# A decoder layer on one core: output sum by pairs of heads, expert weights in a ring of quarters, query and key copies on ScalarE

## The reference, cut to what matters

```python
q = (x @ w_q).reshape(b, n, HEADS, DIM_HEAD).transpose(0, 2, 1, 3)   # 8 heads of 64
k = (x @ w_k).reshape(b, n, HEADS, DIM_HEAD).transpose(0, 2, 1, 3)
gates = jax.nn.sigmoid((x @ w_gate).reshape(b, n, HEADS, EXPERTS).transpose(0, 2, 1, 3))
sel = jnp.argmax(gates, axis=-1)
gm = jax.nn.one_hot(sel, EXPERTS, dtype=x.dtype) * gates
values = jnp.einsum('bhne,ehdk,bnd->bhnk', gm, value_experts, x)
sim = jnp.einsum('bhid,bhjd->bhij', q * SCALE, k)                    # causal mask, then softmax
attn = jax.nn.softmax(sim, axis=-1)
out = jnp.einsum('bhij,bhjk->bhik', attn, values)
out = jnp.einsum('bhne,ehkd,bhnk->bhnd', gm, output_experts, out)
return out.sum(axis=1)
```

## Time and profile before

| | |
|---|---|
| median of 3 runs | 1032.64 us (1027.52 to 1032.67) |
| the profiled execution's own time | 1030.41 us |
| its span | 1028.6 us |
| mean granted TensorE clock | 0.97 |
| TensorE matmuls busy | 932.1 us (91%) |
| VectorE busy | 672.6 us (65%) |
| GpSimd busy | 397.9 us (39%) |
| ScalarE busy | 348.4 us (34%) |
| heads of the third layer | about 251 to 419 and 759 to 918 us |
| output sum | about 420 to 527 and 918 to 1025 us |

### The profile page before, as it was taken

The page is one execution under the profiler, slowest core; times in us unless marked ns, Lnnn a source line. Parts: engine busy times, 40 slices in busy tenths (PEclk is TensorE's granted clock), DMA queues, the critical chain, the costliest instruction groups (busy, mean ns, idle before and its releaser), DMA issues.

```text
span 1028.6 us, 15147 instructions
## 1 busy us (share of the span) xinstructions
PE 932.1 (91%) x5740; PEld 713.0 (69%) x5740; DVE 672.6 (65%) x1032; ACT 348.4 (34%) x634; POOL 397.9 (39%) x365
## 2 busy tenths in 40 slices
PE   6989899998889798689999999999989889885998
PEld 3578588886555455489975777888765556455998
DVE  4767575466455565898869556754754465768887
ACT  4545563111444445201124355610014454541000
POOL 6212231125666667635620032300045664782000
PEclk9999999999889899899999999999989999998999
DMA  6111002532453621445540000022330121131753
GB/s 203 46 63 62 1 1 69 178 100 71 146 162 99 234 59 44 121 150 179 174 134 1 1 1 1 2 89 82 103 103 21 22 60 25 42 94 44 220 178 123
DMA packets 39014, 90.18 MB, mean 88 GB/s; under 512 B 8975, under 2 KB 13775, under 8 KB 38943
## 3 DMA queue, kind: packets, MB, share of 16 engines
q1 hardware_dynamic: 36063, 79.79, 24.9%
q10 hardware_dynamic: 2880, 9.44, 4.0%
HBM read 61.35 MB, written 19.30 MB: 78 GB/s over the span
## 4 chain that ended last, share of the span: by engine, by line
PE 77%; DMA 8%; DVE 8%; issue 3%; ACT 3%; POOL 0%; SPq 0%; ACTq 0%; POOLq 0%; DVEq 0%
PE ps L1254 17%; PE ps L1602 10%; PE ps L1494 5%; PE ps L1478 5%; PE ps L1608 5%; DMA qq<-qq 5%; PE ps L1433 4%; PE ps L1520 4%; PE ps L1262 4%; PE ps L1385 3%; PE ps L1447 3%; PE ps L1400 2%; PE ps L1566 2%; PE ps L1567 2%; PE ps L1296 1%
## 5 line engine op out<-in xcount | busy, mean ns | idle before, releaser
L1116 DVE TENSOR_REDUCE region<-ps 128x1 f32<-128x512 f32 (+1 forms) x192 | 99.0, 551 | 105.1 <-PE ps L1497 102.4
L1602 PE MATMUL ps<-expert_hi,kst 128*128 128x256 f32 x512 | 128.1, 288 | 26.4 <-DVE kst L1200 24.8
L1169 DVE COPY_PREDICATED region<-region,ps 128x512 f32<-128x512 uint32 x112 | 82.0, 736 | 72.2 <-PE ps L1254 71.6
L1602 PE MATMUL ps<-expert_lo,kst 128*128 128x256 f32 x512 | 125.7, 282 | 0.0
L624 POOL TENSOR_TENSOR xT<-xT,region 128x896 f32<-128x896 f32 (+2 forms) x48 | 83.9, 1748 | 92.5 <-PE ps L1520 50.7
L1602 PEld LDWEIGHTS ps<-expert_hi,kst 128*128 128x128 f32 x512 | 98.1, 192 | 30.4 <-DVE kst L1200 22.3
L1254 PE MATMUL ps<-expert_hi,wide_hi 128*128 128x512 f32 x256 | 102.7, 401 | 0.0
L1494 PE MATMUL ps<-kst,qq 128*128 128x512 f32 (+1 forms) x192 | 74.8, 436 | 30.2 <-DMA qq<-qq 30.2
L1254 PE MATMUL ps<-expert_hi,wide_lo 128*128 128x512 f32 x256 | 100.1, 391 | 0.0
L1254 PE MATMUL ps<-expert_lo,wide_hi 128*128 128x512 f32 x256 | 99.8, 390 | 0.0
L1602 PEld LDWEIGHTS ps<-expert_lo,kst 128*128 128x128 f32 x512 | 98.5, 192 | 0.0
(11 more groups left out here) (163 smaller groups left out, 1953.4 us busy)
## 6 DMA issues: line engine op xcount, KB each, us to landing
region<-hot_rows SPq DMA_DIRECT2D x128, 128.0 KB, 3.8
expert_hi<-halves_kept SPq DMA_DIRECT2D x24, 512.0 KB, 3.7
expert_lo<-halves_kept SPq DMA_DIRECT2D x24, 512.0 KB, 5.0
halves_kept<-expert_hi SPq DMA_DIRECT2D x16, 512.0 KB, 5.3
halves_kept<-expert_lo SPq DMA_DIRECT2D x16, 512.0 KB, 6.1
expert<-in_value_experts SPq DMA_DIRECT2D x8, 512.0 KB, 4.3
qq<-qq ACTq DMA_DIRECT2D x16, 256.0 KB, 2.9
kx<-kst ACTq DMA_DIRECT2D x16, 256.0 KB, 3.3
```

The source lines that it names most:

```text
L1116: dve.tensor_reduce(mx[:, i, at_mx:at_mx + 1], ps[:, max_bank(h, m), 0:w], AX.X, ALU.max).then_inc(sem["s_max"], 1)
L1169: dve.copy_predicated(V3_heads[:, t], chosen.unsqueeze(3).broadcast_to([P, PAIRS3, 2, HD3]), ps[:, n % 4, :].rearrange("p (a i k) -> p a i ...
L1602: mm(ps[:, 4 + t // 2, t % 2 * D:(t % 2 + 1) * D], kst[n % 2][:, t * P:(t + 1) * P], w[:, slot, columns], start=(n == 0 and t % 2 == 0 and ...
```

## The change

It has four parts.

1. `SUMMED` goes pair by pair: pair 0 through all 8 experts, then pair 1, and so on. Pair 2's last products with `gb` move between items 0 and 1 and behind item 1, pair 3's work to items 4, 8 and 9, and the rounding of pairs 2 and 3 (`ROUND_LATE_AT`) to items 3, 5, 13 and 15.
2. The output experts come as one quarter of a piece for each item (128x256 of each half, 128 KB), into a ring of 8 quarters in the same two slots.
3. Pair 3's sums are inverted as those of the other pairs, over DRAM. `normalise`, `spread_gates` and the special cases go. SP fetches the first masks ahead of pair 2's factors.
4. `queries_twice` and `keys_twice` are copies on ScalarE out of `raw`. The weighings move: key tile 2 behind block 9 and now ahead of `max_rows`, tiles 3 and 4 behind block 11, tiles 5 to 7 late.

```diff
-    SUMMED = [(0, 0), (0, 1), (0, 2), (1, 0), (1, 1), (0, 3), (1, 2), (1, 3)]
-    SUMMED += [(e, p) for e in range(2, E3) for p in range(PAIRS3)]
+    SUMMED = [(e, p) for p in range(PAIRS3) for e in range(E3)]
+    QUARTERS = SLOTS * PAIRS3
...
-        ROUND_AT = {(5, 4): 0, (5, 6): 1, (6, 4): 2, (6, 6): 3, (7, 9): 4, (7, 11): 5}
+        ROUND_AT = {(5, 4): 0, (5, 6): 1, (6, 4): 2, (6, 6): 3}
+        ROUND_LATE_AT = {3: 4, 5: 5, 13: 6, 15: 7}
...
-        NORMALISED_AFTER = (1, 2, 4)
+        FACTORS_LATE_AT, WEIGHTED_LATE_AT = 4, (8, 9)
+        SUMS_LATE_AT = 1
...
-        PROJECT_AT = (3, 5, 7, 10)
+        PROJECT_AT = (3, 5, 7, 11)
...
-        LATE_AT, SUMS_AT, EARLY_AT, MIDDLE_AT = 1, 6, 6, 9
+        WEIGH_AT = {6: (0, 1), 9: (2,), 11: (3, 4)}
+        LATE_AT, LATE, SUMS_AT = 1, (5, 6, 7), 6
...
+        def item_place(n):
+
+            k = n % QUARTERS
+            return k // PAIRS3, slice(k % PAIRS3 * D, (k % PAIRS3 + 1) * D)
...
+            def fetch_item(b, n):
+
+                (e, p), (slot, columns) = SUMMED[n], item_place(n)
+                for half, w in enumerate((expert_hi, expert_lo)):
+                    sp.dma_start(w[:, slot, columns].bitcast(fp32), halves_kept[E3 + e, half][:, p * D:(p + 1) * D]
+                                 ).then_inc(item_in[n % QUARTERS], 16)
...
+                for n in range(QUARTERS):
+                    piece_used(sp, b, E3 - SLOTS + item_place(n)[0])
+                    fetch_item(b, n)
                 if b:
                     turn_gates(b)
-                for p in range(BY_COLUMNS):
+                for p in range(PAIRS3 - 1):
                     if b + p:
                         keep_den(b, 2 * p)
                         keep_den(b, 2 * p + 1)
                         turn_den(b, p)
+                        if p == PAIRS3 - 2:
+                            until(sp, "kst_ready", b, 2 * H3)
+                            until(sp, "qq_ready", b, 2 * H3)
+                            until(sp, "qx_ready", b, H3)
+                            until(sp, "kx_ready", b, H3)
+                            for n in range(MASKS):
+                                fetch_mask(b, n)
                         spread_factors(b, p)
...
+                keep_den(b, H3 - 2)
                 for n in range(NEP):
+                    if n == SUMS_LATE_AT + 1:
+                        keep_den(b, H3 - 1)
+                        turn_den(b, PAIRS3 - 1)
+                    if n == FACTORS_LATE_AT + 1:
+                        spread_factors(b, PAIRS3 - 1)
                     if n + MASKS < NEP:
                         until(sp, "mo_lo_ready", b, n + 1)
                         fetch_mask(b, n + MASKS)
...
+                    if n >= 2 and n - 2 + QUARTERS < NEP:
+                        until(sp, "mo_used", b, n - 1)
+                        fetch_item(b, n - 2 + QUARTERS)
...
                 def queries_twice(h):
 
                     i, own, oth = h % 2, HALF * (h % 2), HALF * (1 - h % 2)
-                    until(act, "qq_ready", b, h + 1)
-                    act.dma_start(qq[i][oth:oth + HALF, :].bitcast(fp32), qq[i][own:own + HALF, :].bitcast(fp32)
-                                  ).then_inc(qq_in, 16)
+                    copy(qq[i][oth:oth + HALF, :], raw[own:own + HALF, 0, :], "qq_ready")
 
                 def keys_twice(h):
 
                     i, own = h % 2, HALF * (h % 2)
-                    until(act, "kst_ready", b, 2 * h + 1)
-                    act.dma_start(kx[i][own:own + HALF, :].bitcast(fp32), kst[i][own:own + HALF, :].bitcast(fp32)
-                                  ).then_inc(kx_in, 16)
+                    copy(kx[i][own:own + HALF, :], raw[own:own + HALF, 1, :], "kx_ready")
...
-                factors(BY_COLUMNS - 1)
-                weighted(H3 - 4)
-                weighted(H3 - 3)
+                factors(PAIRS3 - 2)
...
                 for n in range(NEP):
                     masked(n)
-                    if n in NORMALISED_AFTER:
-                        normalise(H3 - 2 + NORMALISED_AFTER.index(n))
-                    if n == NORMALISED_AFTER[-1]:
-                        until(dve, "oT_ready", b, len(PARTS))
+                    if n < 2:
+                        weighted(H3 - 4 + n)
+                    if n == FACTORS_LATE_AT:
+                        factors(PAIRS3 - 1)
+                    if n in WEIGHTED_LATE_AT:
+                        weighted(H3 - 2 + WEIGHTED_LATE_AT.index(n))
```

More of the change, by code:

```diff
@@ L59, in decoder_layer @@
     MASKS = 4
-    SUMMED = [(0, 0), (0, 1), (0, 2), (1, 0), (1, 1), (0, 3), (1, 2), (1, 3)]
-    SUMMED += [(e, p) for e in range(2, E3) for p in range(PAIRS3)]
-    LAST_OF = {e: max(n for n, (x, _) in enumerate(SUMMED) if x == e) for e in range(E3)}
+    SUMMED = [(e, p) for p in range(PAIRS3) for e in range(E3)]
+    QUARTERS = SLOTS * PAIRS3
     GW = G + H3
@@ L193, in decoder_layer @@
         gb = sb("gb", [P, S])
-        factors_of = lambda p: gb if p < BY_COLUMNS else xT[:, 0, :]
         hot_T = gb[0:G, :].bitcast(bf16)[:, 0:S]
@@ L405, in turn_gates @@
                 until(sp, "v3_ready", b, TT + 1)
-                for p in range(BY_COLUMNS):
+                for p in range(PAIRS3):
                     sp.dma_start(gate_cols[:, p, :], columns_of(gate_rows[b, 2 * p:2 * p + 2])
@@ L632, in _ @@
                             piece_low(b, E3 + SPLIT_AT[h, n])
-                        if (h, n) in ROUND_AT and h < H3 - 1:
+                        if (h, n) in ROUND_AT:
                             outputs_low(ROUND_AT[h, n])
@@ L853, in den_copy @@
                 def den_copy(h):
[L855 removed]
                     until(act, "den_ps", b, h + 1)
[L857 to L866 removed]
+                    if b or h >= 2:
+                        act.wait_ge(den_kept[h % 2], 16 * (b * PAIRS3 + h // 2))
+                    copy(rden[:, h % 2 * CH:(h % 2 + 1) * CH], ps[:, SUM_BANK[h % 2], :], "den_sb")
                 for q in range(SLOTS, E3 + SLOTS):
@@ L914, in _ @@
                 den_copy(H3 - 1)
-                for k in range(len(ROUND_AT), len(PARTS)):
-                    rounded(k)
                 for n in range(NEP):
+                    if n in ROUND_LATE_AT:
+                        rounded(ROUND_LATE_AT[n])
                     if b + 1 < B and n in APPLY_AT:
@@ L1571, in _ @@
                         if n == LATE_AT and h:
-                            for late in range(TC, TT):
-                                weigh(h - 1, late)
+                            for j in LATE:
+                                weigh(h - 1, j)
                         if n == SUMS_AT and h:
                             denominators(h - 1)
-                        if n == EARLY_AT:
-                            weigh(h, 0)
-                            weigh(h, 1)
+                        for j in WEIGH_AT.get(n, ()):
+                            weigh(h, j)
                         if h + 1 < H3:
@@ L1583, in _ @@
                                 max_rows(h + 1)
-                        if n == MIDDLE_AT:
-                            weigh(h, 2)
-                            weigh(h, 3)
                         if n in PROJECT_AT and h % 2 == 0 and h + 2 < H3:
                             project(h // 2 + 1, PROJECT_AT.index(n))
-                for late in range(TC, TT):
-                    weigh(H3 - 1, late)
+                for j in LATE:
+                    weigh(H3 - 1, j)
                 until(pe, "pt_ready", b, H3 * NB)
                 for n, (e, p) in enumerate(SUMMED):
-                    if p == 0:
-                        piece_here(pe, b, E3 + e)
+                    pe.wait_ge(item_in[n % QUARTERS], 32 * (b * (NEP // QUARTERS) + n // QUARTERS + 1))
                     until(pe, "mo_hi_ready", b, n + 1)
-                    slot, columns = e % SLOTS, slice(p * D, (p + 1) * D)
+                    slot, columns = item_place(n)
                     def high(t):
```

137 lines of the change are left out of this document (43 added, 94 removed).

## The result

The changed kernel took 983.78 us (median of 4 runs, 982.45 to 986.64), the kernel before 1030.42 beside it (4 runs, 1027.52 to 1032.67). The ratio is 0.9553, with a 95% interval from 0.9513 to 0.9592: faster by 46.6 us. The forecast was 979, in 961 to 1006. The profiled execution has a span of 980.6 us (before 1028.6) at a mean granted clock of 0.98 (before 0.97); TensorE's matmuls are busy 924.7 us, 94% of the span.

The account below looks back on a forecast made before the run. Time could be won only in the heads, where scores wait for the queries' DMA, and where heads pass into the sum. Gains of 25 + 27 = 52 us off 1030.4 gave 978, stated as 979, range 961 to 1006.

Parts of the forecast that it names:

- Queries and keys on ScalarE: Heads: ScalarE copies replace DMA copies and shorten the scores' waits, 20.6 us gained, less 2 for late exponentials.
- the head at 347: Stall of 4.83 us before a head's scores: gives back 2.2 us, not 4.5, because of the keys' split.
- Weighings: Heads: a moved weighing fills the wait of the maxima's transpose; from 0 to 7 us, taken as +3.
- Clock: Heads: shorter stalls give back slow-clock time, from 0 to 15 us, taken as +3.
- what is won on one side is mostly waited for at the scores: Heads: weighing 4, about 0.5 us, moves ahead of the next head's block 0, so the 7 us shrinks to +3.
- Heads together: All terms of the heads: 20.6 - 2 + 3 + 3 = 25 us gained.
- The sum's start: Start of the output sum in both sequences: pair 0 first lets item 8 begin earlier, 27 us gained.
- nothing, covered by 15 items of 2.83 us: Output sum: the last pair's small reciprocals, over DRAM at items 4 to 9, needed at item 24, cost nothing.
- then come the sums of head 7, which need GpSimd's last addition: Sum's start, after items 0 and 1: addition ends at 426.07, and about 1.1 us of TensorE gives 427.2.
- Ring of quarters: Output sum: smaller fetches cost nothing, as SP issues an item's four DMAs in 2.06 us, inside 2.83.
- The rival: Output sum: SP cannot issue four DMAs an item in time, the ring starves, 1091 us; chance 0.03.
- the two cases with one gain: Only the sum gains, 1005 us, chance 0.11; or only the heads gain, 1007 us, chance 0.06.

Follow-up runs that it names:

- e3: The changed kernel with queries and keys copied by DMA again and the weighings put back, so only the output sum's parts are new: 1008.52 us.
- e2: The changed kernel with only the weighings and last projection put back at their old places, copies staying on ScalarE: 982.31 us.
- experiment 8: The changed kernel with pairs 0 and 1's products with `gb` moved from ahead of the keys' split to behind maxima 7 and 8: 972.74 us.
- e12: The changed kernel with keys split ahead of products, later roundings, pair 3's spreading and products, but old weighings and last projection: 968.59 us.
- e4: The changed kernel with each quarter's half fetched as two 64 KB DMAs, so SP issues six DMAs an item instead of four: 1046.71 us.

## Why the prediction was right

The two gains, their places and their sign came as forecast, and the time lies 4.8 us above the point. That it lies so near is in part luck: a clock term too small by 5 us and two new waits that the sum put at nothing, or elsewhere, partly cancel. Step by step:

- **Queries and keys on ScalarE, 20.6 us, less 2.** Right in mechanism and nearly in size: 21.6 us of idle time went (`e3` to `e2`). The scores' waits are 0.21 to 0.35 us at ten heads, 1.16 at the one that was at 848 in the earlier trace rows, and 2.5 at three where the keys' split is late. The prediction had the two head 7s as staying and the head at 347 as one that gives back only 2.2 us; the last came so (2.48 us left of 4.83), and the two at head 7 even grew, from 2.01 to 2.52. That they stay was a choice of the order on VectorE, and experiment 8 removed them.
- **Weighings, 3 us.** Wrong in this kernel: 0 to -1.5. The step "the wait is filled, 14 x 0.5 = 7 us" was right, and so was "what is won on one side is mostly waited for at the scores", 3.5 us; the 2.0 us of idle time left over went to the lower clock (2.6 us, `e2` beside the changed kernel), which this term did not have. With the keys in time they may be worth 3 us (`e12`).
- **Clock, 3 us.** Too small. 8.1 us of the heads' gain is shorter busy time, and 8.3 us of the copies' alone. The step that failed is "I take +3, near the lower end": the short waits had no spell to give back, but the long ones of the first sequence had, and 5.9 of the 8.3 us are from there. The Trainium skill, page "TensorE: Matmul & The Clock Gate", part 1, says that activity decides between the levels, and by it the removed stalls would give their spells back; the rows of `e2` and `e3` agree for about half of the 15 us that this would have made.
- **Heads together, 25 us.** 29.6 between the timelines: 21.5 of idle time, where the terms for it add up to 21.6, and 8.1 of clock instead of 3. The medians of the experiments give 26.2 - 1.5 = 24.7.
- **The sum's start, 27 us.** 29.0 from item 0 to item 8, and item 8 stands 24.28 us behind item 0 in both sequences. (2.83 us an item is not 70 us over 24 items, which is 2.92; from item 8 to item 31 the kernel before took 2.88 and 2.80 us an item. It changes the term by tenths.) But "nothing, covered by 15 items of 2.83 us" failed for the last pair's factors. The cover held for TensorE's need at item 24; what was late was SP's queue: `spread_factors` waits there for a store to DRAM, with item 9's masks behind it, and VectorE's products wait for `gb` with item 9's masking behind them. 6.1 us from item 8 to 31. Also "then come the sums of head 7, which need GpSimd's last addition" had the right wait mostly in the wrong stretch: head 7's sums wait 0.5 us for GpSimd, behind item 1, and head 6's wait 1.96 us, in each sequence. By `e3` the sum's parts gave 21.3 us of the 27.
- **Ring of quarters, nothing.** Right: an item takes 2.80 us, SP is through in 2.24. The page "DMA: Bandwidth & Descriptors" of the Trainium skill, section Bandwidth, wants DMAs of 1 MiB. The estimate of 9.2 us an item did not come true; the page gives the fit behind it in another section, "Anatomy of one DMA — SWDGE (gpsimd) path", for single DMAs issued from GpSimd. Here SP issues them, each item's four DMAs lie beside those of other items, and 128 KB landed in 2.8 to 3.3 us. The rival's price held for the sum: it had 3.9 us an item as the point from which the ring costs the whole gain, and at SP's 3.84 the sum of `e4` loses 50.3 us, about the whole gain of 48.0. What makes `e4` slower than before is the stall in the heads, which the rival did not have.
- **Sum.** Predicted 25 + 27 = 52 off the profiled execution, measured 48.0. By the table of stretches: heads 4.6 more than forecast, the sum's start 2.0 more, the holes behind item 8 -6.1, the wait for GpSimd -2.2, and -2.3 in the stretches before head 0's block 1, between the sequences and at the end.
- **The range.** 961 to 1006 was said to take in the two cases with one gain nearly whole, but their own points are 1005 and 1007, so about half of each lies outside. It made no difference here.

## What to carry to other kernels

A step that is wanted late can still be early enough in a queue to stop what stands behind it. For every moved wait, list what follows on its engine and on the queue that issues its DMAs, not only who needs its result. In `e4` the ring's first filling, wanted only in the sum, stopped the heads in the same way. When two engines feed one stalled step, take away both before you judge either: the queries' DMA hid the keys, the spreading hid `gb`. And price a stall with its slow clock, from a stretch with stalls of that length, not from one with short ones.
